# Graph layer with sorted edges: counts on two engines, positions in pieces, masks and first gathers ahead of the collecting group

## The chip, the core and the metric

The kernel runs on one core of a Trainium2 chip: TensorE (PE in the profile) multiplies, VectorE (DVE), ScalarE (ACT) and GpSimd (POOL) work elementwise, SyncE (SP) issues DMAs, and every engine runs its own queue of instructions in order. GpSimd also issues the indirect DMAs: one such instruction moves 128 rows, one a partition, to or from addresses in a column of integers. The metric is the device time of one execution in microseconds (us).

## What is computed

A graph of 6250 nodes with 256 features and 206250 directed edges, one loop per node included, passes through one layer: a graph attention (4 heads), a linear attention over all nodes, and a gated feed-forward with a shared network and the best two of four experts. Cut to the part that matters here:

```python
xn = _layernorm(x)
Wh = (xn @ W.T + b).reshape(N, HEADS, HEAD_DIM)
e = leaky_relu(alpha_src[src] + alpha_dst[dst], 0.2)
ex = exp(e - segment_max(e, src)[src])
att = ex / segment_sum(ex, src)[src]
gnn = segment_sum(att[:, :, None] * Wh[dst], src).reshape(N, 256)
x = x + gnn + mix(xn)
x = x + ffn(_layernorm(x))
```

The kernel sums over the edges that leave a node, so the edges have to stand together by blocks of 128 source nodes; there are NB = 49 blocks.

## The kernel before

**Stage one, sort and mix** (`stage_sort_and_mix`). The edges lie as 128 partitions by TE = 1612. GpSimd makes constants (L258 to L273; the last one signals `s_const`) and fills the list with padding. VectorE turns the source node into its block (`bucket`, L307, L308). In L311 to L315 it counts, for each of the 49 blocks, how many of a partition's edges belong to it: one instruction compares all 1612 entries with the block's number and sums them into a column of `counts`. From these follow the runs of Q = 8 edges that each block gets (L318 to L324), then a bitonic sort of 2048 keys a partition (66 pairs of minimum and maximum, L354, L355). L361 to L371 take the sorted keys apart for all WINDOWS = 244 windows of 8 edges: the window's block (`win_b`) and the payload (target row and source row within the block). L374 to L391 work out, from sums over partitions that TensorE made, how far each block is shifted. L392 to L401 make the positions in four parts of 61 windows: compare with 50 block numbers (L394), multiply by the shifts (L396), sum (L397), add the window's number (L398), turn it into an integer (L400) and signal `s_pos`. GpSimd waits for a part and scatters it, one indirect DMA a window (L283), 244 in all.

Behind the positions VectorE makes tables for the loop (L403 to L452) and then normalises the nodes and takes part in the mix: TensorE, ScalarE and VectorE go through 13 batches of 4 blocks. ScalarE's queue in this stage begins with the copies of turned weights (L545 to L560). A barrier ends the stage: all engines wait until the last scatter has landed.

**Stage two, edges and feed-forward** (`stage_edges_and_feed_forward`). VectorE takes maxima of the scores (L1331 to L1334), GpSimd reduces them over the partitions (L923), VectorE makes a plan from them (L1337 to L1352, `s_plan`). The plan says whether the scores have so wide a spread that extra sweeps are needed; with these inputs there is one collecting group of two gathers (`collect`, L940), whose scores SyncE stores to memory (L878) and loads again (L883, L884) for a single sweep through all engines. SyncE's queue then loads the weights of the feed-forward. VectorE ends the preparation with L1402, which signals `s_ready`.

The loop handles 234 lots of 8 tiles of 128 edges (LOTS = 6 buffers). For each lot GpSimd gathers 8 times 128 rows of 260 numbers from the node table (`gathers`, L928 to L935); it may refill a buffer only when the sums of the lot six before are done (`s_sum`, L929). VectorE makes a one-hot matrix of the edges' source rows (`select`, L1410), TensorE turns it (L979) and looks up scores with it (L989), VectorE and ScalarE make weights of them (L1419 to L1425, L1186), VectorE multiplies the rows by the weights (L1431), and TensorE adds up by node (L1007). Spread over the lots are pieces of dense work: mixing (`mix`) and feed-forward (`piece`), by an order written out in `all_segments` (L826): six lots with the mix of the tail batch, some plain lots, the tail's feed-forward, six lots with the mix of batch 0, plain lots, and so on.

GpSimd's queue in stage two, in order (L921 to L966): all-reduce, wait for the plan, collecting group, gathers of lots 0 to 4, then five instructions that make two masks for the feed-forward (`expert_rows`, `lower`, L948 to L960, signalling `s_set`), a wait for `s_ready`, gathers of lot 5, and the loop. VectorE waits for `s_set` before its first selection, TensorE before its first lot:

```python
            dve.wait_ge(s_set, 2)
            select(0, 0)
            select(0, 1)
            all_segments(dve, lot, piece, mix)
```

## Time and profile before

| | |
|---|---|
| median of 3 runs | 3190.27 us (3189.21 to 3194.09) |
| profiled execution | 3205.1 us |
| its span, first to last instruction | 3203.4 us |
| mean granted TensorE clock | 0.839 of full speed |
| busy: TensorE, VectorE, ScalarE, GpSimd | 2181.0, 1919.5, 753.7, 2163.3 us |
| GpSimd: 244 scatters (L283), 1872 gathers (L933) | 247.1 us, 1904.7 us |
| VectorE: 49 counts (L314) | 88.9 us |

The busy times are sums over the whole span and hide that the stages have different limits. In an answer on waits a row reads: engine, operation and line that waited, what released it, us in total, times, the longest. In a timeline a row reads: start, duration, engine, line, operation, output<-inputs, shapes, count of merged instructions, and in brackets the idle time ahead of it with what ended it. In a group of instructions a row gives the count, the busy time in us, the mean in ns, and the idle time ahead.

### The profile page before, as it was taken

To read this page: it belongs to the slowest core of one execution; us is meant where nothing else is said; L and a number is where in the kernel's file an instruction comes from. 1 tells how busy PE (TensorE), PEld (TensorE's weight loads), DVE (VectorE), ACT (ScalarE), POOL (GpSimd) and SP (SyncE) were. 2 spreads that over 40 slices of the span, in tenths; PEclk is the share of its full clock that TensorE was granted. 3 is DMA by queue.
4 is the path that set the end of the run, shared out by engine and by line. 5 is a ranking of instruction groups with operands and counts; after the bars stand their busy time and mean duration, and the time that the engine had idled before them with its cause. 6 is when DMAs were issued, how large, how long until landed. Compare 5 with 4: busy or idle time off the path is not lost.

```text
span 3203.4 us, 40657 instructions
## 1 busy us (share of the span) xinstructions
PE 2181.0 (68%) x10817; PEld 1528.2 (48%) x10818; DVE 1919.5 (60%) x3954; ACT 753.7 (24%) x1346; POOL 2163.3 (68%) x2140
## 2 busy tenths in 40 slices
PE   0000687037778868787787978878768787787877
PEld 0000454025555555555555655555555555555554
DVE  8999554036565574656666465575654655756563
ACT  0000343012322222222222222222212222222222
POOL 0003777667777777777777777777777777777770
PEclk6555899568898998888889989898989888899988
DMA  5000122143434444444444434434444344344463
GB/s 183 0 0 1 54 72 66 18 118 91 116 92 105 121 102 123 100 110 113 103 122 101 121 103 104 124 101 123 102 105 123 98 111 117 99 124 102 122 93 31
DMA packets 271533, 305.63 MB, mean 95 GB/s; under 512 B 164258, under 2 KB 210856, under 8 KB 271080
## 3 DMA queue, kind: packets, MB, share of 16 engines
q0 software_dynamic: 97760, 251.60, 30.3%
q1 hardware_dynamic: 140098, 18.08, 3.8%
q10 hardware_dynamic: 33480, 33.36, 3.2%
q8 instruction: 122, 2.00, 0.3%
q14 instruction: 73, 0.60, 0.1%
HBM read 276.25 MB, written 26.62 MB: 95 GB/s over the span
## 4 chain that ended last, share of the span: by engine, by line
PE 34%; POOL 23%; issue 11%; DVE 9%; ACT 1%; DMA 1%; POOLq 0%; DVEq 0%; SPq 0%; ACTq 0%
POOL gathered L933 23%; PE sum_banks L1007 18%; PE f_banks L1022 7%; DVE onehot L1410 3%; PE turned L979 2%; PE f_banks L1066 1%; PE f_banks L1141 1%; DVE gathered L1431 1%; PE sum_banks L995 1%; DMA gathered<-table,col 1%; PE f_banks L1047 1%; PE f_banks L1142 1%; PE f_banks L1048 1%; DVE he L1559 1%; DVE he L1562 1%
## 5 line engine op out<-in xcount | busy, mean ns | idle before, releaser
L933 POOL DMA_INDIRECT gathered<-table,col x1872 | 1904.7, 1017 | 594.7 <-issue 564.5
L1007 PE MATMUL sum_banks<-gathered,onehot 128*128 128x260 f32 x3744 | 1060.8, 445 | 103.2 <-DVE gathered L1431 102.5
L1007 PEld LDWEIGHTS sum_banks<-gathered,onehot 128*128 128x128 f32 x3744 | 818.0, 224 | 292.2 <-issue 129.9
L1431 DVE TENSOR_TENSOR gathered<-gathered 128x512 f32<-128x512 f32 x936 | 591.5, 692 | 46.5 <-ACT gathered L1186 43.7
L1410 DVE TENSOR_TENSOR onehot<-iota_row,col 128x1024 f32<-128x1024 f32 x236 | 288.8, 1224 | 476.0 <-PE sum_banks L1007 447.9
L283 POOL DMA_INDIRECT edge_list<-payload,pos x244 | 247.1, 1013 | 349.9 <-DVE pos L400 273.0
L1182 ACT COPY onehot_t<-turned 128x1024 bf16<-128x1024 bf16 x236 | 238.7, 1011 | 398.0 <-PE turned L979 392.0
L1196 ACT COPY acc<-sum_banks x234 | 88.0, 376 | 870.3 <-PE sum_banks L1007 721.2
L979 PE MATMUL turned<-ident_bf,onehot 128*128 128x128 bf16 x1888 | 158.4, 231 | 188.9 <-DVE onehot L1410 188.8
L979 PEld LDWEIGHTS turned<-ident_bf,onehot 128*128 128x128 bf16 x1888 | 116.1, 103 | 207.0 <-DVE onehot L1410 168.9
L989 PE MATMUL scores<-t,onehot_t 128*128 x1880 | 102.2, 175 | 141.8 <-DVE scored L1419 98.8
L989 PEld LDWEIGHTS scores<-t,onehot_t 128*128 128x128 bf16 x1880 | 86.8, 97 | 219.3 <-issue 200.2
L644 PE MATMUL bank<-ident,y 128*128 128x128 f32 x56 | 8.2, 294 | 234.6 <-DVE y L482 234.6
L1419 DVE TENSOR_REDUCE scored<-scores 128x64 f32<-128x192 f32 x234 | 81.8, 350 | 101.3 <-DMA gathered<-table,col 86.0
L995 PE MATMUL sum_banks<-zeros 1*128 1x260 bf16 x236 | 70.6, 300 | 99.2 <-issue 92.2
L644 PEld LDWEIGHTS bank<-ident,y 128*128 128x128 f32 x56 | 7.0, 153 | 235.3 <-issue 235.3
L1022 PE MATMUL f_banks<-xT,wT_mix 128*128 128x512 f32 x208 | 94.9, 599 | 16.5 <-ACT xT L1294 16.5
L995 PEld LDWEIGHTS sum_banks<-zeros 1*128 1x128 bf16 x236 | 21.7, 92 | 166.2 <-issue 157.7
L1022 PE MATMUL f_banks<-xT,eW 128*128 128x512 f32 (+1 forms) x208 | 90.2, 568 | 0.0
L314 DVE TENSOR_SCALAR_CACHE_REDUCE xn_all<-xn_all,iota_row 128x1612 bf16<-128x1612 bf16 x49 | 88.9, 1891 | 1.8 <-POOL ones_row L273 1.8
L1219 ACT ACTIVATE he<-f_banks,eb 128x512 f32<-128x512 f32 (+1 forms) x78 | 51.3, 661 | 139.1 <-PE f_banks L1022 134.4
L354 DVE TENSOR_TENSOR xn_all<-xn_all 128x1024 f32<-128x1024 f32 x66 | 80.9, 1226 | 2.3
(316 smaller groups left out, 2499.8 us busy)
## 6 DMA issues: line engine op xcount, KB each, us to landing
gathered<-table,col POOLq DMA_INDIRECT x1872
xn_batch<-xn ACTq DMA_DIRECT2D x13, 512.0 KB, 4.4
x_all<-in_x SPq DMA_DIRECT2D x1, 6144.0 KB
x_batch<-in_x ACTq DMA_DIRECT2D x12, 512.0 KB
out<-xf ACTq DMA_DIRECT2D x12, 512.0 KB
edge_list<-xn_all SPq DMA_DIRECT2D x2, 2176.0 KB, 13.7
edge_list<-payload,pos POOLq DMA_INDIRECT x244
col<-edge_list SPq DMA_DIRECT2D x236, 8.0 KB, 2.1
```

Source lines behind the costliest of these rows:

```text
L283: g.indirect_dma_start(sh["windows"], bass.IndirectOffsetOnAxis(ap=pos[:, w:w + 1], axis=0), payload[:, w * Q:w * Q + Q, :].rearrange("p e ...
L314: v.tensor_scalar(hit[b % 2], bucket, iota_row[:, b:b + 1], 0.0, ALU.is_equal, ALU.add, accum_out=counts[:, b:b + 1]).then_inc(s_counts, 1)
L933: g.indirect_dma_start(gathered[:, l, t, :], None, sh["table"], bass.IndirectOffsetOnAxis(ap=col[l][:, t // G, t % G, 0:1], axis=0)).then_ ...
L979: last = t.transpose(turned[:, tile * P:tile * P + P], halves_of[:, l % 3, tile, :, 1], ident_bf[:, :])
L989: last = t.matmul(scores[:, tile * PIECE:tile * PIECE + PIECE], onehot_t[:, l % 2, tile, :], t24[:, ds(blocks[tile // G], 1), :].rearrange ...
L995: return t.matmul(sum_banks[:, bank, 0:TB].rearrange("p a w -> p (a w)"), zeros[:, 0:P], zeros[:, :], start=True, stop=False, skip_group_c ...
L1007: last = t.matmul(sum_banks[:, ds(banks_of[g], 1), 0:TB].rearrange("p a w -> p (a w)"), onehot[:, l % 3, g * G + k, :], gathered[:, l, g * ...
L1022: last = t.matmul(bank, left, right, start=i == 0, stop=i == len(pairs) - 1)
L1182: s.copy(onehot_t[:, l % 2, :, :].rearrange("p t e -> p (t e)"), turned[:, :]).then_inc(s_ot, 1)
L1196: s.copy(acc[:, ds(place, 1), :], sum_banks[:, ds(bank, 1), 0:TB]).then_inc(s_cp, 1)
L1410: v.tensor_tensor(onehot[:, l % 3, :, :], iota_row[:, :].unsqueeze(1).broadcast_to([P, TILES, P]), within.broadcast_to([P, TILES, P]), ALU ...
L1431: v.tensor_tensor(value, value, gathered[:, l, tiles, C:TB].unsqueeze(3).broadcast_to([P, G, H, HD]), ALU.mult).then_inc(s_mul, 1)
```

## The change

The counts of blocks 0 to 24 stay on VectorE. ScalarE takes 25 values, for b = 24 to 48: the sum over the edges of the sign of b + 0.5 - bucket, whose difference from one b to the next is twice the count; VectorE takes the differences and halves them. ScalarE's two scratch outputs lie where the sort's first buffer begins. The payload and the positions are made in five pieces, of 16 and four times 57 windows, each with its own taking apart of keys, so that the first piece is ready earlier and the taking apart moves behind the shifts. GpSimd makes one constant more (`edge_of`) ahead of `s_const`. In stage two GpSimd makes the masks at the very start of its queue, and gathers lot 0 ahead of its wait for the plan and the collecting group.

```diff
-PART, PARTS = WINDOWS // 4, 4
+FIRST_PART, PART = 16, 57
+PART_ENDS = (FIRST_PART, *range(FIRST_PART + PART, WINDOWS + 1, PART))
+ON_ACT = 24
...
+        above = [keys[0][:, i * (TE // 2):(i + 1) * (TE // 2)].bitcast(BF16) for i in range(2)]
...
+            step(g.tensor_scalar(edge_of[:, :], iota_row[:, 0:NB], 0.5, None, ALU.add))
             step(g.iota(key_of[:, :], [[1, NB]], base=0, channel_multiplier=0))
...
             for w in range(WINDOWS):
-                if w % PART == 0:
-                    pool.wait_ge(s_pos, w // PART + 1)
+                if w == 0 or w in PART_ENDS:
+                    pool.wait_ge(s_pos, 1 + sum(end <= w for end in PART_ENDS))
...
             step(v.tensor_copy(bucket, int_tmp))
+            v.memset(balance[:, 0:ON_ACT], 0.0).then_inc(s_bucket, 1)
 
             dve.wait_ge(s_const, 1)
-            for b in range(NB):
+            for b in range(ON_ACT + 1):
...
-            dve.wait_ge(s_counts, NB)
+            dve.wait_ge(s_counts, ON_ACT + 1)
+            dve.wait_ge(s_balance, NB - ON_ACT)
+            rising = slice(ON_ACT + 1, NB)
+            step(v.tensor_tensor(counts[:, rising], balance[:, rising], balance[:, ON_ACT:NB - 1], ALU.subtract))
+            step(v.tensor_scalar(counts[:, rising], counts[:, rising], 0.5, None, ALU.mult))
...
-            entries = keys[0][:, 0:WINDOWS * Q].bitcast(I32)
-            other = keys[1][:, 0:WINDOWS * Q]
-            v.tensor_scalar(win_i[:, :], entries.rearrange("p (w e) -> p w e", e=Q)[:, :, 0], 20, DEAD,
...
-            for part in range(PARTS):
-                mine = slice(part * PART, (part + 1) * PART)
...
+            for part, end in enumerate(PART_ENDS):
+                first = PART_ENDS[part - 1] if part else 0
+                some, mine, edges = end - first, slice(first, end), slice(first * Q, end * Q)
+                entries, other = keys[0][:, edges].bitcast(I32), keys[1][:, edges]
+                v.tensor_scalar(win_i[:, mine], entries.rearrange("p (w e) -> p w e", e=Q)[:, :, 0], 20, DEAD,
+                                ALU.logical_shift_right, ALU.bitwise_and)
+                v.tensor_scalar(payload[:, edges, 0], entries, (1 << 13) - 1, None, ALU.bitwise_and)
+                step(v.tensor_scalar(other.bitcast(I32), entries, 13, P - 1, ALU.logical_shift_right, ALU.bitwise_and))
+                v.tensor_copy(win_b[:, mine], win_i[:, mine])
+                step(v.tensor_copy(payload[:, edges, 1].bitcast(F32), other.bitcast(I32)))
+                step(v.tensor_scalar(win_b[:, mine], win_b[:, mine], float(NB), None, ALU.min))
+                step(v.tensor_scalar(other, payload[:, edges, 0], float(NO_TARGET), NO_NODE, ALU.is_ge, ALU.mult))
+                step(v.tensor_tensor(payload[:, edges, 1].bitcast(F32), payload[:, edges, 1].bitcast(F32), other, ALU.add))
+                of, place = lookup[:, 0:some, :], pos_f[:, 0:some]
+                step(v.tensor_tensor(of, win_b[:, mine].unsqueeze(2).broadcast_to([P, some, NBK]),
+                                     iota_row[:, 0:NBK].unsqueeze(1).broadcast_to([P, some, NBK]), ALU.is_equal))
+                step(v.tensor_tensor(of, of, shift[:, :].unsqueeze(1).broadcast_to([P, some, NBK]), ALU.mult))
+                step(v.tensor_reduce(place, of, AX.X, ALU.add))
+                step(v.scalar_tensor_tensor(place, place, float(first), iota_row[:, 0:some], ALU.add, ALU.add))
+                v.tensor_copy(pos[:, mine], place).then_inc(s_pos, 1)
                 dve.wait_ge(s_pos, part + 1)
...
         @block.scalar
         def _(act):
             s = nc.scalar
+            act.wait_ge(s_const, 1)
+            act.wait_ge(s_bucket, 1)
+            for b in range(ON_ACT, NB):
+                i = b - ON_ACT
+                if i >= 2:
+                    act.wait_ge(s_balance, i - 1)
+                s.activation(above[i % 2], bucket, ACT.Sign, bias=edge_of[:, b:b + 1], scale=-1.0,
+                             accum_out=balance[:, b:b + 1]).then_inc(s_balance, 1)
...
         @block.gpsimd
         def _(pool):
             g = nc.gpsimd
+            g.memset(expert_rows[:, :], 1.0).then_inc(s_pool, 1)
+            pool.wait_ge(s_pool, 1)
...
+            g.affine_select(out=lower[:, :, :], in_=lower[:, :, :], compare_op=ALU.is_gt, fill=0.0, base=0,
+                            pattern=[[1, NE], [-1, NE]], channel_multiplier=0).then_inc(s_set, 1)
             pool.wait_ge(s_max, 2)
             g.partition_all_reduce(ad_top[:, :], ad_max[:, :], P, sh["RMAX"]).then_inc(s_top, 1)
...
+            gathers(0, 0)
             pool.wait_ge(s_plan, 1)
             collect(pool, sweep_gathers)
-            for l in range(LOTS - 1):
+            for l in range(1, LOTS - 1):
                 gathers(0, l)
-            g.memset(expert_rows[:, :], 1.0).then_inc(s_pool, 1)
-            pool.wait_ge(s_pool, 1)
...
             pool.wait_ge(s_ready, 1)
             gathers(0, LOTS - 1)
```

## Rows read from the trace of the kernel before

**Rows 1.** VectorE's waits, 550 to 700 us.

```profile
DVE gathered L1331 <- PEq L100: 67.6, 1, 67.6
DVE onehot L1410 <- POOL lower L959: 27.9, 1, 27.9
```

**Rows 2.** GpSimd's waits, 684 to 800 us and 830 to 976 us.

```profile
POOL gathered L933 <- PE sum_banks L1007: 16.4, 6, 5.3
...
POOL gathered L933 <- PE sum_banks L1007: 10.5, 4, 5.6
```

**Rows 3.** VectorE's timeline, the first count and the instruction behind the last.

```profile
12.41 1.89 DVE L314 TENSOR_SCALAR_CACHE_REDUCE xn_all<-xn_all,iota_row 128x1612 bf16<-128x1612 bf16 x1 [1.81 <-POOL ones_row L273]
...
101.37 0.19 DVE L318 TENSOR_SCALAR runs<-counts 128x49 f32<-128x49 f32 x1
```

**Rows 4.** ScalarE's groups of instructions, shapes kept apart, whole span.

```profile
L1182 ACT COPY onehot_t<-turned 128x1024 bf16<-128x1024 bf16 x236 | 238.7, 1011 | 398.0 <-PE turned L979 392.0 <-issue 5.5
...
L575 ACT COPY xT<-bank 128x512 f32<-128x512 f32 x14 | 7.5, 589 | 5.5 <-PE bank L644 5.5
```

**Rows 5.** VectorE's timeline, from the end of the sort to the first part.

```profile
266.59 0.38 DVE L363 TENSOR_SCALAR xn_all<-xn_all 128x244 int32<-128x244 int32 x1
266.89 1.17 DVE L365 TENSOR_SCALAR payload<-xn_all 128x1952 int32<-128x1952 int32 x1
...
272.12 2.19 DVE L371 TENSOR_TENSOR payload<-payload,xn_all 128x1952 f32<-128x1952 f32 x1
...
277.68 3.34 DVE L394 TENSOR_TENSOR xn_all<-xn_all,iota_row 128x3050 f32<-128x3050 f32 x1
```

**Rows 6.** Timeline at the first scatters, and the scatters' group from 266 to 320 us.

```profile
289.21 3.58 POOL L283 DMA_INDIRECT edge_list<-payload,pos  x1 [273.03 <-DVE pos L400]
...
293.09 2.72 POOL L283 DMA_INDIRECT edge_list<-payload,pos  x1 [0.30 <-issue]
295.01 3.33 DVE L397 TENSOR_REDUCE xn_all<-xn_all 128x61 f32<-128x3050 f32 x1
296.11 0.96 POOL L283 DMA_INDIRECT edge_list<-payload,pos  x1 [0.30 <-issue]
...
L283 POOL DMA_INDIRECT edge_list<-payload,pos x15 | 27.4, 1825 | 277.3 <-DVE pos L400 273.0 <-issue 4.3
```

**Rows 7.** Timeline of stage two up to the first selection.

```profile
617.32 0.49 DVE L1334 TENSOR_REDUCE ad_max<-gathered 128x4 f32<-128x196 f32 x1
...
622.64 0.39 POOL L923 PARTITION_ALL_REDUCE ad_top<-ad_max  x1 [9.41 <-issue]
...
629.59 1.19 POOL L940 DMA_INDIRECT gathered<-table,sweep_col  x1 [6.56 <-DMA sweep_col<-edge_list]
...
632.33 0.94 POOL L933 DMA_INDIRECT gathered<-table,col  x1 [0.30 <-issue]
...
655.82 0.09 DVE L1402 MEMSET den<- 128x32 f32 x1
...
682.20 0.30 POOL L948 MEMSET expert_rows<- 5x256 f32 x1
682.57 0.39 POOL L951 TENSOR_SCALAR_AFFINE_SELECT expert_rows<-expert_rows 5x256 f32<-5x256 f32 x1
...
683.81 2.36 DVE L1410 TENSOR_TENSOR onehot<-iota_row,col 128x1024 f32<-128x1024 f32 x2 [27.91 <-POOL lower L959]
```

**Rows 8.** GpSimd's timeline at the start.

```profile
8.43 0.28 POOL L259 TENSOR_SCALAR_AFFINE_SELECT ident<-ident 128x128 f32<-128x128 f32 x1 [7.40 <-issue]
...
11.35 0.18 POOL L267 IOTA key_of<- 128x49 int32 x1
```

**Rows 9.** Loop: a gather, a reduction of scores, and all gathers from 976 to 3134 us.

```profile
899.25 1.52 POOL L933 DMA_INDIRECT gathered<-table,col  x1 [5.57 <-PE sum_banks L1007]
...
976.29 0.36 DVE L1419 TENSOR_REDUCE scored<-scores 128x64 f32<-128x192 f32 x1 [2.82 <-DMA gathered<-table,col]
...
L933 POOL DMA_INDIRECT gathered<-table,col x1631 | 1660.5, 1018 | 496.9 <-issue 493.6 <-PE sum_banks L1007 3.4
```

More of the change, by code:

```diff
@@ L73 @@
 assert ITERS % 2 == 1
-assert TE + PAD_SLOTS <= SLOTS and WINDOWS == PART * PARTS and GR % Q == 0
+assert TE + PAD_SLOTS <= SLOTS and WINDOWS == PART_ENDS[-1] and GR % Q == 0
 assert NO_TARGET == 52 * P and NB * P <= 1 << 13 and NO_TARGET < 1 << 13
@@ L133, in stage_sort_and_mix @@
         key_of = sb("key_of", [P, NB], I32)
+        edge_of = sb("edge_of", [P, NB])
+        balance = sb("balance", [P, NB])
         lives = sb("lives", [P, NB, Q - 1], BF16)
@@ L195, in stage_sort_and_mix @@
         s_scat = (s_scat0, s_scat1)
+        s_bucket, s_balance = sem("s_bucket"), sem("s_balance")
         s_bias, s_bias_out, s_ad = sem("s_bias"), sem("s_bias_out"), sem("s_ad")
@@ L359, in _ @@
             assert now == 0
-            entries = keys[0][:, 0:WINDOWS * Q].bitcast(I32)
-            other = keys[1][:, 0:WINDOWS * Q]
-            v.tensor_scalar(win_i[:, :], entries.rearrange("p (w e) -> p w e", e=Q)[:, :, 0], 20, DEAD,
-                            ALU.logical_shift_right, ALU.bitwise_and)
-            v.tensor_scalar(payload[:, :, 0], entries, (1 << 13) - 1, None, ALU.bitwise_and)
-            step(v.tensor_scalar(other.bitcast(I32), entries, 13, P - 1, ALU.logical_shift_right, ALU.bitwise_and))
-            v.tensor_copy(win_b[:, :], win_i[:, :])
-            step(v.tensor_copy(payload[:, :, 1].bitcast(F32), other.bitcast(I32)))
-            step(v.tensor_scalar(win_b[:, :], win_b[:, :], float(NB), None, ALU.min))
-            step(v.tensor_scalar(other, payload[:, :, 0], float(NO_TARGET), NO_NODE, ALU.is_ge, ALU.mult))
-            step(v.tensor_tensor(payload[:, :, 1].bitcast(F32), payload[:, :, 1].bitcast(F32), other, ALU.add))
             dve.wait_ge(s_base, 1)
@@ L391, in _ @@
             step(v.tensor_scalar(shift[:, NB:NBK], node_col[:, :], float(WINDOWS), float(LIST // Q), ALU.mult, ALU.add))
-            for part in range(PARTS):
-                mine = slice(part * PART, (part + 1) * PART)
-                step(v.tensor_tensor(lookup, win_b[:, mine].unsqueeze(2).broadcast_to([P, PART, NBK]),
-                                     iota_row[:, 0:NBK].unsqueeze(1).broadcast_to([P, PART, NBK]), ALU.is_equal))
-                step(v.tensor_tensor(lookup, lookup, shift[:, :].unsqueeze(1).broadcast_to([P, PART, NBK]), ALU.mult))
-                step(v.tensor_reduce(pos_f[:, :], lookup, AX.X, ALU.add))
-                step(v.scalar_tensor_tensor(pos_f[:, :], pos_f[:, :], float(part * PART), iota_row[:, 0:PART],
-                                            ALU.add, ALU.add))
-                v.tensor_copy(pos[:, mine], pos_f[:, :]).then_inc(s_pos, 1)
+            for part, end in enumerate(PART_ENDS):
[18 more added lines that the diff above has]
+                v.tensor_copy(pos[:, mine], place).then_inc(s_pos, 1)
@@ L921, in _ @@
             g = nc.gpsimd
+            g.memset(expert_rows[:, :], 1.0).then_inc(s_pool, 1)
+            pool.wait_ge(s_pool, 1)
+            g.affine_select(out=expert_rows[:, :], in_=expert_rows[:, :], compare_op=ALU.is_ge, fill=0.0, base=0,
+                            pattern=[[1, NE * EH2]], channel_multiplier=-EH2).then_inc(s_pool, 1)
+            pool.wait_ge(s_pool, 2)
+            g.affine_select(out=expert_rows[:, :], in_=expert_rows[:, :], compare_op=ALU.is_gt, fill=0.0, base=EH2,
+                            pattern=[[-1, NE * EH2]], channel_multiplier=EH2).then_inc(s_set, 1)
+            g.memset(lower[:, :, :], 1.0).then_inc(s_pool, 1)
+            pool.wait_ge(s_pool, 3)
+            g.affine_select(out=lower[:, :, :], in_=lower[:, :, :], compare_op=ALU.is_gt, fill=0.0, base=0,
+                            pattern=[[1, NE], [-1, NE]], channel_multiplier=0).then_inc(s_set, 1)
             pool.wait_ge(s_max, 2)
```

9 lines of the change are left out of this document (removed).

## The prediction

> **What bounds the kernel now.** I read the waits of VectorE and GpSimd first, then the timeline around each long wait, then the groups of instructions for prices. The kernel has two stages with a barrier between them at about 616 us. In the first, VectorE counts, sorts and makes positions alone until 289.21 us, when GpSimd starts its 244 scatters [rows 6]; it ends with GpSimd, for VectorE stands 67.6 us at the barrier [rows 1]. So the path is VectorE's work up to the first positions, and then the scatters one after the other. In the second stage VectorE's first selection of a lot waits 27.9 us for the masks that GpSimd writes only after forty gathers [rows 1]. Then comes the loop over 234 lots. From 976 us on GpSimd hardly ever waits for TensorE (3.4 us in all), while VectorE waits for gathers [rows 9]: GpSimd's stream sets the end. Before that GpSimd waited for the sums, 16.4 us in 6 waits and 10.5 us in 4 [rows 2]; there the consumers (VectorE, TensorE, ScalarE on a lot) set it. The sum is made against the profiled execution, 3205.1 us (its span of 3203.4 and 1.7 around it); it stands 14.8 us above the median of the runs, 3190.27, and I take the same saving off the median. Under 0.2%, 6.4 us, a measurement of this kernel can't tell a difference from none.
>
> **Counts.** The 49 counts run from 12.41 to 101.37 us [rows 3], 1.815 us each. Taken off VectorE: 24, or 43.6 us. The 25 left end 45.4 us after their start. ScalarE gets 25. No row has it reading 1612 elements: its bf16 copy of 1024 takes 1.011 us and its copy of 512 takes 0.589 [rows 4], 0.824 ns per element, so 1.50 us for 1612, and some 0.1 to 0.2 to write out a sum: 1.65 each, 41 us, done 4 us ahead of VectorE. I cost it at nothing; its cover is VectorE's own 25 counts, gone when ScalarE's price passes 1.815 us. Lower bound 1.3 (the cheaper copy's rate), which gains nothing more; upper 2.1 (three waits of 0.2 added), which is 7.1 us late. I stand near the copies, since they are the same engine at the same type. ScalarE's weight copies, queued behind the counts, come some 40 us later; nothing on the path reads them before the mix, which VectorE starts only after all positions. Added on the path: two small VectorE instructions at the 0.19 of a 49-column one [rows 3] with their gaps, 0.45; GpSimd's edge_of ahead of the constants that VectorE already waits 1.81 us for [rows 3], 0.25 by the 49-column iota [rows 8]. VectorE's zeroing of balance lies in that wait. **42.9 us saved.**
>
> **Positions in pieces.** Ahead of the first scatter, the preparation of all 244 windows (266.59 to 274.31) and a part of 61 windows (277.68 to 289.21) [rows 5, 6] leave: 7.7 + 11.5. In their place stand eight preparations of 16 windows, 128 edges, at 0.19 to 0.28 each, 1.8 in all; three passes over 800 elements at 0.95 (3.34 for 3050 [rows 5], on a floor of 0.1), two small ones and gaps, 3.4; and the release of GpSimd, 1.0. The first scatter comes 13.0 us earlier. A later piece takes VectorE some 12.8 us, and 16 scatters at 0.96 + 0.30 [rows 6] last 20, so GpSimd doesn't run dry.
> Against that, a cost. While VectorE runs its two products with two SBUF operands (L394, L396) scatters take 3.58 and 2.72 us; beside the reduction they take 0.96 [rows 6]. The 15 scatters beside three parts took 27.4, 13.0 more than 15 x 0.96 [rows 6], 4.3 a part. Now four parts of 57 windows run beside scatters instead of three of 61: 4 x 4.05 = 16.2. Their preparations, which ran beside no scatter before, last 2.8 us a piece: between 0 and 2.8 lost each. I take 0.5, since they are short (0.4 each, after L365's 1.17 for 1952) and between two of them a scatter can start. Together 18.2 against 13.0: 5.2 lost. **7.8 us saved net**; bounds -1.4 and 9.8.
> The Trainium skill ("SBUF — State Buffer", Who interferes with whom) says that VectorE and GpSimd share a port pair under an exclusive lock: two-input instructions contend with GpSimd's reads, copies, casts and tensor_scalars can too, reductions never. By that rule the trace agrees on the products and the reduction; on the preparations no row shows it.
>
> VectorE itself ends its mix later against the sort by some 6 us of small instructions; of the 67.6 us it had to spare [rows 1] about 50 stay. GpSimd's last scatter stays the end, 50.7 us earlier.
>
> **Masks and first gathers ahead.** The masks' five GpSimd instructions (682.20 to 683.78 [rows 7]) move to the stage's start, beside VectorE's maxima, which end at 617.81 [rows 7]: GpSimd is ready for the all-reduce some 0.3 us later. Lot 0's eight gathers move into GpSimd's idle 6.56 us ahead of the collecting group [rows 7]; at 0.94 + 0.30 [rows 7] they need 10.0, so they push that group's two gathers back 4.0. The list columns that they wait for are loaded at the stage's start, so that wait costs nothing. Behind the collecting gathers stand SyncE's store and reload of scores, its queue of weight loads, and through them all engines: the ready point at 655.9 [rows 7] goes to 660.2. The last gather lot waits for it on GpSimd, but is due only at about 676. The first selection, which now waits for the ready point instead of GpSimd, goes from 683.81 [rows 7] to 660.2: 23.6 us earlier.
> GpSimd's stream: lot 1 starts 5.9 us earlier (from 632.33 + 10.0 to 623.3 + 0.3 + 10.0 + 2.5 + 0.3), and the 1.9 us of masks leave. Consumers 23.6 us ahead remove most of its first 16.4 us of waits. By the gather at 899.25, which waited 5.57 for sums [rows 9], GpSimd alone could be 5.9 + 1.9 + 16.4 + 10.5 = 34.7 us earlier; the sums it waits for are only 23.6 earlier. The later of the two decides: **23.6 us saved**, carried through the GpSimd-bound rest.
>
> Sum: 42.9 + 7.8 + 23.6 = 74.3. Profiled 3130.8; median **3116.0**.
>
> **Rivals.**
> (a) The consumers' head start is lost, because the lots wait for gathers instead: only GpSimd's 5.9 of the 23.6 stays, 3133.7. For it: the loop later waits for gathers [rows 9]. Against: 26.9 us of waits the other way [rows 2]. 0.12.
> (b) ScalarE's count costs the 2.1 us of the bound: 7.1 late, 3123.1. 0.09.
> (c) Code has to be brought in again for the moved masks or for edge_of: GpSimd stood 7.40 us ahead of its first affine select [rows 8], while at 682.57 such an instruction followed without a pause [rows 7]. 3123.4. Beside this, the Trainium skill ("GPSIMD Engine Reference", Instruction dispatch) says that a freshly loaded kernel's first call pays some 6 us that no instruction shows. 0.07.
> (d) The preparations hold every scatter for all their time: 4 x 2.3 more, 3125.2. The page named above would have it so. 0.05.
> (e) The counts aren't shared in effect: two engines reading one tensor hold each other so that 25 take what 49 took. From 3.5 us a count on; 42.9 lost, 3158.9. 0.04.
> (f) Slower: the gathers fall differently beside VectorE's two-operand instructions. The 1631 after 976 us average 1.018 us [rows 9] against 0.94 unhindered [rows 7]; if the new phase lifts that by 0.05 the saving is gone, and at 1.08 (a further hold of 0.25 us at every fourth gather) the time is 3217. It ends slower from 1.068 on. Against: where GpSimd is the bound the consumers follow its landings, so the phase sets itself. 0.03.
>
> **How the numbers follow.** Forecast 0.60, the rivals as given. Range 3103 to 3135: below by what the loop's holds may give back (0.008 us a gather, 13 us), above to take in (a) to (d); it leaves out (e), (f) and the tails. Faster by over 0.2%: 0.95, nearly all but (f); within: 0.02; slower: 0.03.
>
> **What would show it.** L314 25 times and ScalarE's counts at about 1.65, done before them; the first scatter near 233 us; two slow scatters in each of four pieces; VectorE's wait at the barrier near 50; the first selection right behind the ready point, some 44 us after the stage's start; GpSimd's waits for sums gone before the first dense piece and some 10 us left before the end of the first full mix. Wrong if ScalarE's counts pass 1.8 us, if GpSimd pauses several us ahead of edge_of, the masks or the all-reduce more than before, or if the gathers' mean moves by more than 0.01.

## The result, and the profile after

The changed kernel takes 3116.75 us (median of 4 runs, 3109.34 to 3119.02), the kernel before 3191.26 in the same session (3189.21 to 3194.09). The ratio is 0.976, with a 95% interval from 0.974 to 0.978. That is 74.5 us less; the forecast was 74.3.

| | before | after |
|---|---|---|
| profiled execution, us | 3205.1 | 3118.8 |
| its span | 3203.4 | 3117.0 |
| counts complete | 101.37 | 58.56 |
| first scatter | 289.21 | 233.12 |
| last scatter ends | 613.23 | 559.87 |
| VectorE's wait at the barrier | 67.6 | 51.8 |
| first selection of a lot | 683.81 | 607.54 |
| last gather starts | 3132.03 | 3044.31 |

The counts first, which answer to [rows 3, 4]. The timelines of ScalarE and VectorE in the changed kernel, at the first and the last count of each (start us, us, engine, line, operation, out<-in, shapes, and in brackets the idle time before with what ended it):

```profile
10.72 1.28 ACT L561 ACT_TABLE_LOAD   x1 [10.57 <-DVE balance L316]
...
12.68 1.64 ACT L561 ACTIVATE xn_all<-xn_all,edge_of 128x1612 bf16<-128x1612 bf16 x1 [0.68 <-POOL ones_row L280]
14.23 0.18 ACT L561 ACTIVATION_READ_ACCUMULATOR xn_all<-xn_all,edge_of 128x1 f32 x1
14.32 1.62 ACT L561 ACTIVATE xn_all<-xn_all,edge_of 128x1612 bf16<-128x1612 bf16 x1
...
53.15 0.18 ACT L561 ACTIVATION_READ_ACCUMULATOR xn_all<-xn_all,edge_of 128x1 f32 x1
...
58.01 0.08 DVE L322 DVE_READ_ACCUMULATOR xn_all<-xn_all,iota_row 128x1 f32 x1
58.13 0.18 DVE L327 TENSOR_TENSOR counts<-balance 128x24 f32<-128x24 f32 x1
...
58.56 0.19 DVE L330 TENSOR_SCALAR runs<-counts 128x49 f32<-128x49 f32 x1
```

From one ACTIVATE to the next ScalarE takes 1.62 us; the separate instruction that reads out the sum lies beside the next count. Its last sum stands at 53.33, VectorE's own last at 58.09, and VectorE goes on 0.04 us later: ScalarE's share is covered. The first row is ScalarE's load of the table for the sign, 1.28 us; it ends at 12.01, ahead of the constants that both engines wait for.

The scatters, against [rows 6]. GpSimd's timeline at the first ones, then VectorE's two products over 2850 elements beside them:

```profile
233.12 1.30 POOL L290 DMA_INDIRECT edge_list<-payload,pos  x1 [216.48 <-DVE pos L411]
234.72 0.98 POOL L290 DMA_INDIRECT edge_list<-payload,pos  x1 [0.30 <-issue]
236.01 2.86 POOL L290 DMA_INDIRECT edge_list<-payload,pos  x1 [0.30 <-issue]
239.18 2.85 POOL L290 DMA_INDIRECT edge_list<-payload,pos  x1 [0.30 <-issue]
```

```profile
234.91 3.13 DVE L406 TENSOR_TENSOR xn_all<-xn_all,iota_row 128x2850 f32<-128x2850 f32 x1
238.07 3.13 DVE L408 TENSOR_TENSOR xn_all<-xn_all,shift 128x2850 f32<-128x2850 f32 x1
```

The first lies beside the preparation of the next piece. The second starts 0.19 us ahead of the first product and takes 0.98, though 0.80 us of it lies beside that product. The third and fourth start within the two products and take 2.86 and 2.85: each ends 0.83 us behind the product in which it began. The later pieces repeat this.

The second stage, against [rows 7]. Timelines of GpSimd and VectorE from its start to the first selection:

```profile
563.22 0.30 POOL L941 MEMSET expert_rows<- 5x256 f32 x1 [3.34 <-POOLq L102]
...
564.10 0.48 DVE L1354 TENSOR_REDUCE ad_max<-gathered 128x4 f32<-128x196 f32 x1
...
564.58 0.23 POOL L952 TENSOR_SCALAR_AFFINE_SELECT lower<-lower 128x16 f32<-128x16 f32 x1
571.02 0.40 POOL L955 PARTITION_ALL_REDUCE ad_top<-ad_max  x1 [6.21 <-issue]
571.61 1.27 POOL L965 DMA_INDIRECT gathered<-table,col  x1 [0.20 <-issue]
...
581.93 0.95 POOL L972 DMA_INDIRECT gathered<-table,sweep_col  x1 [0.30 <-issue]
...
607.50 0.09 DVE L1422 MEMSET den<- 128x32 f32 x1
607.54 1.23 DVE L1430 TENSOR_TENSOR onehot<-iota_row,col 128x1024 f32<-128x1024 f32 x1
```

The first selection (L1430) now stands directly behind the ready point (L1422), where it had waited 27.9 us for the masks [rows 1]. In front of the all-reduce are 6.21 us in which GpSimd waits for nothing shown, and they begin only when the masks are done: more on that below.

Later GpSimd hardly waits. Its waits for sums (engine, line, releaser: us in total, times, longest) from 608 to 724 us and from 754 to 900, the stretches of [rows 2] moved by the 76 us of the lead, were 16.4 and 10.5 us before:

```profile
POOL gathered L965 <- PE sum_banks L1027: 1.2, 4, 0.3
...
POOL gathered L965 <- PE sum_banks L1027: 3.7, 3, 3.1
```

The profiled pair is 86.3 us apart and not 74.5. Up to the first selection it is 76.3; from there to the last gather the execution before took 2448.2 us (3132.03 - 683.81) and the one after 2436.8, 11.4 less, and behind the last gather 71.4 and 72.7. Most of the 11.4 is no step of the change: the repetition below took 2444.5 us on this way.

### The profile page after: what moved, and what is told of

Same layout as the page of the kernel before. It is cut to its first block, busy times and chain, and to the rows that moved or that the text cites. A ratio compares the mean times of both kernels' runs of the same rounds, so it can differ in the third digit from the quotient of the medians.

```text
span 3117.0 us, 40701 instructions
## 1 busy us (share of the span) xinstructions
PE 2181.7 (70%) x10817; PEld 1529.3 (49%) x10818; DVE 1882.2 (60%) x3946; ACT 792.2 (25%) x1396; POOL 2160.0 (69%) x2141
## 4 chain that ended last, share of the span: by engine, by line
PE 50%; DVE 14%; issue 8%; POOL 6%; ACT 2%; DMA 1%; ACTq 0%; DVEq 0%; POOLq 0%; SPq 0%; another core or an unknown queue 0%
PE sum_banks L1027 26%; PE f_banks L1042 9%; POOL gathered L965 6%; DVE onehot L1430 5%; PE turned L999 3%; PE f_banks L1161 2%; DVE gathered L1451 2%; PE f_banks L1086 1%; PE sum_banks L1015 1%; PE f_banks L1067 1%; PE f_banks L1162 1%; DVE he L1579 1%; DVE he L1582 1%; PE f_banks L1068 1%; ACT onehot_t L1202 1%
## 5 line engine op out<-in xcount | busy, mean ns | idle before, releaser
L965 POOL DMA_INDIRECT gathered<-table,col x1872 | 1898.4, 1014 | 572.9 <-issue 563.2
L1430 DVE TENSOR_TENSOR onehot<-iota_row,col 128x1024 f32<-128x1024 f32 x236 | 288.9, 1225 | 448.4 <-PE sum_banks L1027 448.0
L290 POOL DMA_INDIRECT edge_list<-payload,pos x244 | 249.9, 1024 | 293.4 <-DVE pos L411 216.5
L1550 DVE TENSOR_TENSOR xf<-x_batch,f_banks 128x256 f32<-128x256 f32 x49 | 20.5, 420 | 105.7 <-PE f_banks L1068 105.7
```

The source lines that it names most:

```text
L290: g.indirect_dma_start(sh["windows"], bass.IndirectOffsetOnAxis(ap=pos[:, w:w + 1], axis=0), payload[:, w * Q:w * Q + Q, :].rearrange("p e ...
L965: g.indirect_dma_start(gathered[:, l, t, :], None, sh["table"], bass.IndirectOffsetOnAxis(ap=col[l][:, t // G, t % G, 0:1], axis=0)).then_ ...
L1430: v.tensor_tensor(onehot[:, l % 3, :, :], iota_row[:, :].unsqueeze(1).broadcast_to([P, TILES, P]), within.broadcast_to([P, TILES, P]), ALU ...
```

## The experiments

Differences are to the changed kernel's medians, 3116.75 in the first session and 3118.67 in a later one (below).

**1. All counts back on VectorE.**

```diff
-            for b in range(ON_ACT + 1):
+            for b in range(NB):
...
-            dve.wait_ge(s_balance, NB - ON_ACT)
-            rising = slice(ON_ACT + 1, NB)
-            step(v.tensor_tensor(counts[:, rising], balance[:, rising], balance[:, ON_ACT:NB - 1], ALU.subtract))
-            step(v.tensor_scalar(counts[:, rising], counts[:, rising], 0.5, None, ALU.mult))
```

ScalarE's loop is taken out too.

> The changed kernel with all 49 counts on VectorE again (ScalarE counts nothing; edge_of is still made). Theory: the counts set the start of the sort, and everything behind them moves with it: the last count ends about 101.3 us instead of 58.0, the first scatter starts at 275.9 instead of 233.1, the first selection comes 42.8 us later, and the time is 3116.7 + 42.8 = 3159.5 us (ratio to the kernel before 0.990). Rival (the edge columns or ScalarE's weight copies would hold the stage anyway once the counts are short, so part of the 42.8 us is not the counts'): the time comes back by less than 35 us, below 3152.

```profile
275.82 1.30 POOL L290 DMA_INDIRECT edge_list<-payload,pos  x1 [259.66 <-DVE pos L407]
```

Measured: first scatter at 275.82 in GpSimd's timeline, 42.7 later; first selection at 649.82, 42.3 later; 3158.47 us (3151.56 to 3161.24), 41.7 slower, ratio to before 0.990. The theory holds: the whole of the counts' time is on the path.

**2. More counts on ScalarE.** `ON_ACT = 16` in place of 24: 33 on ScalarE, 17 on VectorE.

> The changed kernel with 33 counts on ScalarE and 17 on VectorE. Theory (a ScalarE count costs 1.62 us whatever VectorE does, and the later of the two engines sets the sort's start): VectorE's counts end at 43.5, ScalarE's last sum at 66.3 instead of 53.3, the subtraction waits for it, the first scatter starts 8.2 us later at 241.3, and the time is 3124.9 us. Rival (two engines reading one tensor hold each other, so that ScalarE's counts run faster once VectorE is done): ScalarE's counts after 44 us take under 1.5 us, and less than 5 us are lost, under 3121.7.

The waiting instruction in VectorE's timeline, and ScalarE's last sum ahead of it:

```profile
43.30 0.08 DVE L322 DVE_READ_ACCUMULATOR xn_all<-xn_all,iota_row 128x1 f32 x1
...
65.90 0.19 ACT L561 ACTIVATION_READ_ACCUMULATOR xn_all<-xn_all,edge_of 128x1 f32 x1
...
66.19 0.19 DVE L327 TENSOR_TENSOR counts<-balance 128x32 f32<-128x32 f32 x1 [22.82 <-ACT xn_all L561]
```

ScalarE's count takes 1.62 us before 43 us and after, so the engines don't hold each other, and the cover ends where the sum said. First scatter 241.2, first selection 615.83 (8.3 later), last gather 3052.43 (8.1 later). The time is 3120.12 (3118.73 to 3124.79), only 3.4 more, ratio 0.978 (0.976 to 0.980). That number lies on the rival's side (under 3121.7), though the rival's mechanism did not come: the loss of 8.3 is plain at the first selection, and further on it lies within what executions differ by. Behind the last gather this execution took 65.2 us and the changed kernel's 72.7, and in the repetition of experiment 9 the changed kernel's last gather, at 3051.78, was nearly as late.

**3. Pieces undone.** Preparation of all windows ahead, four parts of 61.

```diff
-FIRST_PART, PART = 16, 57
+FIRST_PART, PART = 61, 61
...
+            v.tensor_scalar(payload[:, :, 0], entries, (1 << 13) - 1, None, ALU.bitwise_and)
...
             for part, end in enumerate(PART_ENDS):
...
-                v.tensor_scalar(payload[:, edges, 0], entries, (1 << 13) - 1, None, ALU.bitwise_and)
```

> The changed kernel with the preparation of all 244 windows ahead of the positions and four parts of 61 windows, as before. Theory (preparations hold no scatter; only the two products with two operands hold, two scatters each piece): first scatter 13.3 us later, at 246.4, and 2.7 us of holds less, so the last scatter ends 10.6 us later, at 570.5, and the time is 3127.3 us. Rival (preparations hold scatters for their 2.8 us a piece, so the pieces give most of their lead back): the last scatter ends at most 4 us later than in the changed kernel, time below 3121.

GpSimd's timeline, first scatters and the last:

```profile
246.45 3.57 POOL L290 DMA_INDIRECT edge_list<-payload,pos  x1 [229.72 <-DVE pos L413]
250.32 2.73 POOL L290 DMA_INDIRECT edge_list<-payload,pos  x1 [0.30 <-issue]
...
569.84 0.96 POOL L290 DMA_INDIRECT edge_list<-payload,pos  x1 [0.31 <-issue]
```

First scatter 13.3 later, last end 10.9 later (570.80 against 559.87); time 3130.09 (3126.3 to 3133.27), 13.3 slower. The theory's 10.6 is nearer than the rival's 4.

**4. Which VectorE instructions hold a scatter.** Extra work on scratch behind the last piece (`flat` is the scratch as one row of 2850 elements, `one` and `two` are its halves):

```diff
...
+            step(v.memset(flat, 1.0))
+            for i in range(4):
+                step(v.tensor_scalar(flat, flat, 1.0, None, ALU.mult))
+            for i in range(3):
+                step(v.tensor_copy(two, one))
+                step(v.tensor_copy(one, two))
+            for i in range(3):
+                step(v.tensor_tensor(flat, flat, flat, ALU.mult))
+            for i in range(2):
+                step(v.tensor_reduce(pos_f[:, 0:1], flat, AX.X, ALU.add))
```

> The changed kernel with 16 more VectorE instructions on scratch, behind the last piece and beside GpSimd's scatters: a memset and four tensor_scalars over 2850 fp32 elements, six fp32 copies of 1425, three products with two operands over 2850, two reductions over 2850. Theory (only instructions with two SBUF operands hold a scatter): scatters beside the products take 2 us or more, those beside memset, tensor_scalars, copies and reductions 0.95 to 1.0; the last scatter ends 2 to 6 us later, since VectorE has 51.8 us to spare at the barrier. Rival (copies and tensor_scalars hold GpSimd as well, and the preparations only escaped because they are short): scatters beside the tensor_scalars and copies take 1.3 us or more each, and the last scatter ends 8 us later or more.

VectorE's timeline of the extra work (a row with x4 is four instructions), then GpSimd's beside it:

```profile
283.62 2.43 DVE L417 MEMSET xn_all<- 128x2850 f32 x1 [0.66 <-DVE pos L411]
286.09 6.87 DVE L419 TENSOR_SCALAR xn_all<-xn_all 128x2850 f32<-128x2850 f32 x4
292.99 0.90 DVE L421 COPY xn_all<-xn_all 128x1425 f32<-128x1425 f32 x1
...
298.62 9.45 DVE L424 TENSOR_TENSOR xn_all<-xn_all 128x2850 f32<-128x2850 f32 x3
308.11 6.28 DVE L426 TENSOR_REDUCE xn_all<-xn_all 128x1 f32<-128x2850 f32 x2
```

```profile
285.51 0.96 POOL L290 DMA_INDIRECT edge_list<-payload,pos  x1 [0.31 <-issue]
286.78 2.94 POOL L290 DMA_INDIRECT edge_list<-payload,pos  x1 [0.30 <-issue]
290.02 3.05 POOL L290 DMA_INDIRECT edge_list<-payload,pos  x1 [0.30 <-issue]
293.38 1.57 POOL L290 DMA_INDIRECT edge_list<-payload,pos  x1 [0.30 <-issue]
...
299.01 3.57 POOL L290 DMA_INDIRECT edge_list<-payload,pos  x1 [0.30 <-issue]
302.88 2.86 POOL L290 DMA_INDIRECT edge_list<-payload,pos  x1 [0.30 <-issue]
...
309.21 0.96 POOL L290 DMA_INDIRECT edge_list<-payload,pos  x1 [0.30 <-issue]
```

My theory falls and the rival holds. Beside the memset and the reductions a scatter takes 0.96, beside products 2.85 to 3.57, but beside fp32 tensor_scalars 2.94 and 3.05 and beside copies 1.57. The last scatter ended 12.9 us later and the one time was 3130.6. The steps are regular: one scatter for each product (both every 3.16 us), one for every two copies (0.94 each; a scatter every 1.87) and one for every two tensor_scalars (1.72 each; scatters end at 289.72 and 293.07, just behind the second and the fourth). So a scatter seems to need VectorE out of the way once beside a product and twice beside the others. The Trainium skill ("SBUF — State Buffer", Who interferes with whom) says that copies and tensor_scalars in a fast mode take both the read and the write port that GpSimd uses, a two-input instruction the read port alone; these steps agree. The same section of the Trainium skill infers that two-input instructions leave GpSimd's writing of descriptors alone and so don't stall its DMAs; the 2.86 us beside products differ, and the measurement decides.

**5. The second stage's order undone.** Masks and lot 0's gathers behind the collecting group, as before.

```diff
-            g.memset(expert_rows[:, :], 1.0).then_inc(s_pool, 1)
...
             pool.wait_ge(s_max, 2)
...
-            gathers(0, 0)
             pool.wait_ge(s_plan, 1)
             collect(pool, sweep_gathers)
-            for l in range(1, LOTS - 1):
+            for l in range(LOTS - 1):
                 gathers(0, l)
+            g.memset(expert_rows[:, :], 1.0).then_inc(s_pool, 1)
...
             pool.wait_ge(s_ready, 1)
```

> The changed kernel with GpSimd's order of the second stage as before (masks and lot 0's gathers behind the collecting group). Theory (the consumers' start sets the time): the first selection comes 23.0 us later against the stage's start, at 630.5, GpSimd waits again about 16 us for sums before lot 12 and another 5 near lot 23, and the time is 3139.7 us. Rival (the head start is lost later, since the lots wait for gathers anyway; only GpSimd's earlier start of lot 1 and the masks' 1.6 us count): 3116.7 + 6 to 8 = 3123 to 3125.

```profile
569.29 0.39 POOL L942 PARTITION_ALL_REDUCE ad_top<-ad_max  x1 [9.47 <-issue]
576.39 1.19 POOL L959 DMA_INDIRECT gathered<-table,sweep_col  x1 [6.71 <-DMA sweep_col<-edge_list]
...
602.20 0.09 DVE L1421 MEMSET den<- 128x32 f32 x1
630.69 2.36 DVE L1429 TENSOR_TENSOR onehot<-iota_row,col 128x1024 f32<-128x1024 f32 x2 [28.40 <-POOL lower L978]
```

In these rows of GpSimd's and VectorE's timelines the selection waits 28.40 us for the masks again. Time 3136.75 (3132.94 to 3139.49), 20.0 slower; from 560 to 900 us GpSimd waited 22.9 us in 8 waits for sums. The theory (23.0) is near, the rival's 6 to 8 falls: the consumers' lead is kept to the end. From the first selection to the last gather this execution took 2437.1 us, the changed kernel's 2436.8.

**6. Masks ahead alone**, with `gathers(0, 0)` behind the collecting group.

> The changed kernel with only the masks ahead; lot 0's gathers stand behind the collecting group as before. Theory (the masks carry the whole gain of the new order, the early gathers only push the collecting group back): the collecting gathers come about 4 us earlier than in the changed kernel, the ready point at 603.5 instead of 607.5, the first selection right behind it or behind lot 0's landing; lot 1 starts 2.5 us later than in the changed kernel; time 3113 to 3119 us, no difference that can be told. Rival (the early gathers carry the gain): the first scored lot comes 6 us or more later than in the changed kernel, and the time is 3123 or more.

```profile
603.99 1.23 DVE L1429 TENSOR_TENSOR onehot<-iota_row,col 128x1024 f32<-128x1024 f32 x1
```

Measured: collecting gather at 578.12 (3.8 earlier), ready point 603.95 (3.6 earlier), first selection 603.99 in VectorE's timeline, with no wait ahead of it. Lot 1 started at 590.84, 6.4 us later and not the 2.5 expected, and the loop did not feel it: the first lot's scores were taken up by VectorE 3.5 us earlier, at 608.63. Time 3114.5 (3113.52 to 3116.38), 2.2 less, ratio 0.976 (0.974 to 0.977). No difference can be told.

**7. First gathers ahead alone**, with the masks behind lots 1 to 4.

> The changed kernel with lot 0's gathers ahead of the collecting group, and the masks behind lots 1 to 4 as before. Theory (the masks are what the first selection waited for; the early gathers help it only by the 5 to 6 us by which lots 1 to 4 are issued earlier): the masks end about 624, the first selection stands right behind them at 624.4 instead of 607.5, and the time is 3116.7 + 16.9 = 3133.6 us, near the kernel with the old order. Rival (the early gathers carry a share of their own, since the loop is bound by gathers later): 3125 or less.

```profile
605.93 0.09 DVE L1422 MEMSET den<- 128x32 f32 x1
624.37 2.36 DVE L1430 TENSOR_TENSOR onehot<-iota_row,col 128x1024 f32<-128x1024 f32 x2 [18.35 <-POOL lower L979]
```

VectorE's timeline: the selection waits 18.35 us for the masks and starts at 624.37, where expected. Time 3132.13 (3130.93 to 3132.88). So from the old order (3136.75) the masks alone bring 22.3 us, the gathers alone 4.6, both 20.0: the masks carry that part of the change. The 4.6 is not clear of the scatter (ratios 0.980 to 0.983 against 0.981 to 0.984); in the traces the first selection came 6.3 us earlier.

**8. The pause in front of the all-reduce.** An additional one in the first stage:

```diff
+            step(g.partition_all_reduce(warm[:, :], ones_sq[:, 0:2 * H], P, sh["RMAX"]))
             pool.wait_ge(s_filled, 32)
```

> The changed kernel with one more all-reduce over partitions, of 8 columns of ones into a scratch, in the first stage, where GpSimd waits for edges and positions anyway. Theory A (the 6.2 us in front of the all-reduce of the second stage are the first use of its code, and the code then stays): the new all-reduce has such a pause in front of it at about 20 us, hidden; the one of the second stage follows VectorE's maxima without a pause, at about 565 instead of 571.0; the first selection comes 6 us earlier, 3110.7 us. Theory B (the code is brought in each time the program turns from other instructions to the all-reduce): 6.2 us stand in front of both, and the time stays 3116.7, or grows by 6 where the masks' instructions have to be brought in again.

GpSimd's timeline: the early all-reduce, the last mask, the second stage's all-reduce.

```profile
25.17 0.39 POOL L284 PARTITION_ALL_REDUCE warm<-ones_sq  x1 [8.56 <-issue]
...
564.74 0.23 POOL L954 TENSOR_SCALAR_AFFINE_SELECT lower<-lower 128x16 f32<-128x16 f32 x1
564.96 0.37 POOL L957 PARTITION_ALL_REDUCE ad_top<-ad_max  x1
```

Theory A is right about the pause: it belongs to the first use, is hidden there, and the second all-reduce follows the masks without one. The first selection came at 602.1, 5.4 earlier. Yet the time is 3116.0 (3114.49 to 3120.15), no better. The gathers' own line shows a loss (minimum, median and maximum ns of one), here and, second, in the changed kernel:

```profile
L967 POOL DMA_INDIRECT gathered<-table,col x1872: 949/953/2004, 566.2 to 3049.2; - x188
```

```profile
L965 POOL DMA_INDIRECT gathered<-table,col x1872: 942/946/1994, 571.6 to 3044.3; - x188
```

The shortest and the median gather take 7 ns more, which would be 13 us over 1872; added up, all gathers took 1908.5 us against 1898.4, 10.1 more. Lot 24 still started 5.4 us earlier than in the changed kernel, lot 225 4.5 later. Against the repetition in experiment 9, where all gathers took 1899.5 us, lot 225 was 1.7 us earlier: that the gathers are slower is plain, but that they took the whole head start rests on the one pair of executions.

**9. The same kernel again, and what beats it.** Three kernels in one session: the changed kernel unaltered, a better order with 26 counts on ScalarE, and that with the early all-reduce. In the better order the all-reduce stands first, the masks right behind it, and only four of lot 0's gathers ahead of the collecting group. The better order with the old 25 counts ("alone") ran in a session of its own.

```diff
-ON_ACT = 24
+ON_ACT = 23
...
+            pool.wait_ge(s_max, 2)
+            g.partition_all_reduce(ad_top[:, :], ad_max[:, :], P, sh["RMAX"]).then_inc(s_top, 1)
             g.memset(expert_rows[:, :], 1.0).then_inc(s_pool, 1)
...
-            pool.wait_ge(s_max, 2)
-            g.partition_all_reduce(ad_top[:, :], ad_max[:, :], P, sh["RMAX"]).then_inc(s_top, 1)
...
-            gathers(0, 0)
+            gathers(0, 0, range(4))
             pool.wait_ge(s_plan, 1)
             collect(pool, sweep_gathers)
+            gathers(0, 0, range(4, TILES))
```

> The changed kernel once more, unaltered, as the measure for the two kernels beside it and for how far its executions scatter. Theory (the start of the loop is the same to 0.1 us in each execution and the scatter comes from the last 70 us, where TensorE's granted clock differs): first selection at 607.5, the last gather starts between 3042 and 3047, the stretch behind it takes 65 to 73 us; median 3114 to 3119. Rival (the scatter lies in the loop's holds): the last gather differs by over 5 us from the earlier execution's 3044.3.

> The changed kernel with 26 counts on ScalarE and 24 on VectorE, the masks right behind the all-reduce, four of lot 0's gathers ahead of the collecting group and four behind it. Theory: the sort starts 1.8 us earlier (VectorE's counts end at 56.2, ScalarE's sums at 55.0); the all-reduce's 6.2 us begin 1.6 earlier, at the stage's start; masks and four gathers fill GpSimd's idle 6.7 us, so the collecting gathers start about 576.5 - 1.8 and the ready point and first selection come 5.4 + 1.8 earlier, about 600.3; lot 1's gathers 1.8 earlier, since GpSimd's stream has no idle time in either kernel. The loop is GpSimd's after lot 24, so the end gains 1.8 and the last of GpSimd's waits (3.1): 3112 to 3115 us. Rival (the consumers' start still sets the end): all 7.2 us, 3109.5.

> The kernel with 26 counts on ScalarE, masks behind the all-reduce and lot 0's gathers split, and with the early all-reduce of the first stage as well. Theory (with no code brought in during the second stage each gather takes 0.953 us instead of 0.946, as in the kernel with the early all-reduce alone): the first selection comes another 5.4 us earlier, about 595, the median gather again 0.953, 13 us more over 1872, and the time is 3111 to 3117, no better than without the early all-reduce. Rival (the slower gathers came from the order of masks and all-reduce, or by chance): the median gather is 0.946 again and the time is 5 us below that of the kernel without the early all-reduce.

> The changed kernel with its own 25 counts on each engine, but with the masks right behind the all-reduce and lot 0's gathers split, four ahead of the collecting group and four behind it. Theory (the consumers' start sets the end): first selection about 602, 5 us earlier than in the changed kernel, and the time between 3108 and 3113 us, that of the kernel with 26 counts on ScalarE plus 1.8. Rival (GpSimd's stream sets the end, and lot 1's gathers start no earlier than in the changed kernel): 3116 to 3119 us, as the changed kernel, so that the gain seen with 26 counts was the counts' and a favourable set of executions.

| | ratio to before (95%) | median, us | first selection | selection to last gather | behind it |
|---|---|---|---|---|---|
| changed kernel again | 0.977 (0.975 to 0.978) | 3118.67 | 607.28 | 2444.5 | 65.4 |
| better order, 26 counts | 0.973 (0.972 to 0.975) | 3107.49 | 601.14 | 2445.9 | 66.7 |
| and early all-reduce | 0.977 (0.975 to 0.978) | 3117.16 | 596.58 | 2447.2 | 69.5 |
| better order alone | 0.974 (0.973 to 0.976) | 3113.59 | 603.28 | 2440.5 | 68.5 |

The first two columns are of all runs, the last three of the profiled execution (the last gather's start less the first selection's, and the span's end less the last gather's start).

The changed kernel repeated to 0.3 us up to the first selection, then lost 7.5 us on the way to the last gather and won 7.3 behind it. So my theory, that executions differ only in the last 70 us, falls: they differ in both. One place in each is plain in the stretches of the two executions (stretch, its length, busy time and instructions of PE, PEld, DVE, ACT and POOL, then TensorE's granted clock, DMA share and GB/s); first the execution shown above, then the repetition:

```profile
687.00:727.00 40.00, 28.96 (x191) 22.62 (x190) 28.65 (x58) 11.51 (x20) 30.86 (x31) 0.95 0.40 103
...
3104.00:3117.00 13.00, 9.16 (x19) 5.03 (x17) 1.26 (x3) 0.00 (x0) 0.00 (x0) 0.50 0.12 40
```

```profile
687.00:727.00 40.00, 29.32 (x173) 22.89 (x173) 25.33 (x52) 9.06 (x17) 30.67 (x30) 0.87 0.39 99
...
3104.00:3117.00 13.00, 9.31 (x34) 5.32 (x32) 2.96 (x6) 0.00 (x0) 0.00 (x0) 1.00 0.12 40
```

Between 687 and 727 us the clock granted to TensorE was 0.95 in the one and 0.87 in the other, between its two levels of 1.2 and 2.4 GHz on average; VectorE took up lot 9's scores 3.8 us later in the other, and that one waited 5.57 us for sums ahead of lot 23 where the first waited 3.07. At the very end the clock stood at the lower level, 0.50, in the one and at the upper, 1.00, in the other, after 20 us of a fully busy TensorE in both. That the clock made these differences is not shown; it only stands beside them.

The better order with 26 counts is 11.2 us faster than the changed kernel beside it, and the intervals don't overlap. That is more than the theory's 2 to 5 us and more than the rival's 7.2, with a first selection 6.1 us earlier. The better order alone (3110.05 to 3117.41) is 5.1 below the changed kernel's 3118.67 of the other session and 0.6 above what its theory allowed, and its interval overlaps the changed kernel's. Both fit a consumers' start that sets the end rather than GpSimd's stream, but the overlap leaves that not shown, and the size beyond 7 us stays unexplained. The profiled execution of the faster kernel was its slowest (3115.39, of 3105.01 to 3115.39). Its trace shows a place where such an execution loses time, GpSimd's waits for sums from 900 us on:

```profile
POOL gathered L966 <- PE sum_banks L1029: 13.1, 15, 4.4
```

Of these, 9.7 us lie ahead of lots 101, 119, 137 and 155; in the two executions of the changed kernel no wait of that stretch lasted over 0.3 us. Whether the faster executions were spared them is not on record.

With the early all-reduce the first selection came 4.6 us earlier still, the median gather took 0.953 again, and the time was 9.7 longer. All gathers together took 1901.7 us against 1893.9, 7.8 more, which less the 4.6 leaves 3.2; the rest is not in this pair of traces, of the slowest run of the one kernel and the fastest of the other.

## Why the prediction was right, and where it was not

**Counts, 42.9: 42.8** (101.37 to 58.56), and 41.7 when undone. ScalarE's estimate of 1.65 measured 1.62, done 4.8 us ahead of VectorE (4 predicted), so rival (b) did not come. That it came so near is in part luck: the slope of 0.824 ns was drawn through a bf16 copy and an fp32 one [rows 4], and the table load of 1.28 us, which the forecast left out, happened to lie ahead of the constants. Reading out the sum costs no pace of its own. `edge_of` took 0.40 instead of 0.25, without a pause ahead of it: rival (c) fell, for the masks too. The first count started 0.28 us later. Rival (e) fell with experiment 2.

**Pieces: 10.6 saved for 7.8 forecast.** The start was 13.3 earlier for 13.0. The term that was mis-sized is the holds, 2.7 for 5.2 (all scatters took 249.9 us, 247.1 before). "I take 0.5" for the preparations: scatters beside them took 0.96 to 1.01, so nearly nothing. And a pair of slow scatters, put at 4.05 a piece, lost 3.8 (2.86 + 2.85 less 2 x 0.96). A little went the other way: the first scatter of all took 1.30, 0.3 more than the rest, with no product beside it. That 0.3 is in the 27.4 of [rows 6] and was not put into the sum for the pieces. Rival (d) fell, though its rule is sound: experiment 4 shows that such instructions do hold GpSimd when they last 0.9 us or more. Why those of 0.4 us did not is open; they differ in type too (integers and casts), and no run separates the two. In three pieces the scatter starts within 0.01 us of the piece's first preparation, so one phase alone was seen.

**Masks and first gathers: 22.9 for 23.6.** (76.3 at the first selection, less 53.4 at the last scatter.) The step that failed is "ready for the all-reduce some 0.3 us later": it is 1.7 (571.02 against 569.29 with the old order and the same stage's start), all of the masks' time. I read the pause ahead of the all-reduce [rows 7] as a wait for VectorE's maxima with room beside it. It is a time of its own, about 6.2 us from when GpSimd comes to the instruction, and what is put ahead of it pushes it back. So the ready point moved by 5.0 and not 4.3. The Trainium skill ("GPSIMD Engine Reference", Instruction dispatch) has the first call of a freshly loaded kernel pay some 6 us that no instruction shows; the 6.21 here agrees, and so does its absence once the early all-reduce has been run. The other mis-judged half: the gathers ahead, on which I spent 4.0 us, bring nothing once the masks are ahead (experiment 6).

**The rest of the way.** "Carried through" held: rival (a) would have lost 17.7 us, and undoing the order cost 20.0. GpSimd's waits ahead of the first dense piece went from 16.4 us [rows 2] to single waits of 0.3. The "some 10 us left" were 3.1 in the profiled execution and 10.5 in the repetition (0.96, 2.20, 1.75 and 5.57 ahead of lots 19, 20, 22 and 23). The gathers' mean, 1.018 before [rows 9], is 1.013 from 890 us on, so rival (f) did not come; but a change of 7 ns a gather, which experiment 8 brought about, ate up about the head start it was traded for.

**The sum** 42.8 + 10.6 + 22.9 = 76.3 stands against 74.3 forecast, and 74.5 in the medians; two errors, 2.8 too little for the pieces and 0.7 too much for the order, were small and of opposite sign. Undone one by one, the three parts cost 41.7, 13.3 and 20.0 us, 75.0 together, so they add up. That forecast and medians agree to 0.2 us is luck: the runs of the changed kernel alone span 9.7 us. The profiled time came out at 3118.8, not 3130.8: the execution before was 14.8 us above its median and the one after 2, and I took the same saving off both.

## What to carry to other kernels

When two engines can share a row of equal instructions, the split is a division of measured paces, and the gain is on the path only as long as the next stage waits for it; undo it once to see that it does. Ahead of a stage's first result, look for what the consumers wait for last: here five short mask instructions stood behind forty gathers and cost 22 us, and the eight gathers moved with them brought nothing. On an engine that issues the loop's DMAs, price a change by what it does to one DMA times their number: 7 ns a gather, some 10 us in all, cancelled a head start of 5.4.

## What the runs showed of the hardware that was not expected

- A scatter that began within a product of two operands (2850 or 3050 elements) ended 0.83 us behind that product's end, in 24 of 25 cases in three traces (before, after and experiment 4); the other was the first scatter of the kernel before, 1.17 behind. One that began 0.19 to 0.26 us ahead of a product took 0.96 to 1.01 us, nearly as if alone.
- Beside fp32 tensor_scalars of 1.72 us a scatter of GpSimd took 2.94 to 3.05 us, beside copies of 0.90 us 1.57, beside memset and reductions 0.96; integer and casting preparations of 0.4 us held it by 0.05 at most, in the one phase that was seen.
- With an all-reduce in the first stage the second stage's all-reduce lost its 6.2 us pause and took 0.37 instead of 0.40, but the median gather took 0.953 us instead of 0.946 and the shortest 0.949 instead of 0.942 or 0.940, in two kernels with two different orders of masks and all-reduce; the scatters of the first stage stayed at 0.958. The cause was not tried.
- Two executions of one kernel, 0.3 us apart at the first selection, were 7.5 us apart at the last gather and 0.2 at the end, with TensorE's granted clock at 0.50 and 1.00 in the last 13 us.
